# Weight pieces and context rows fetched on GpSimd's queue in the cross stage, and rounded in later slots

## The chip, the cores and the metric

The kernel runs on one core of a Trainium2 chip. A core has TensorE (matmuls into PSUM), VectorE, ScalarE, GpSimd, and SyncE (SP), which here only issues DMAs; the engines run by themselves and meet at semaphores. DMAs issued by SP and by GpSimd are moved by the same 16 DMA engines. The metric is the device time of one execution in microseconds (us). Runs of the kernel before took 1236.08, 1238.08 and 1243.37 us, a median of 1238.08.

## The reference

A decoder layer over x, 16 sequences of 128 rows and 512 columns, in float32:

```python
x = x + attn(layernorm(x))            # 16 query heads of 128, one key/value head, causal, rotary
x = x + xattn(layernorm(x), ctx)      # 8 heads of 16 over the 512 positions, band of 64 either way
x = x + ffn(layernorm(x))             # quantised linear layers with a gate

# xattn, per sequence: x is used as (128 features, 512 positions)
q, k, v = split(x.T @ w_in.T + b_in)
p = softmax(where(band, q @ k.T / sqrt(16), -big))
y = relu((p @ v) @ w_out.T + b_out).T * ctx      # ctx: the context rows of this sequence
out = w_ct.T @ y + b_ct

# ffn: both weight matrices are quantised to -1, 0, 1
scale = 1 / max(mean(abs(w)), 1e-5)
wq = clip(round(w * scale), -1, 1) / scale
```

## The kernel before, in words

The kernel has three stages: attention (to about 622 us of the span), the cross stage (to about 1022 us), and the feed-forward stage. Every stage is a software pipeline over the 16 sequences, written out by hand.

The cross stage (`cross`, L953 on) runs `step(b)` for b from -3 to 18 on each engine, and in each step 8 slots, s = 0 to 7. One step does different work for several sequences: maximum scores of sequence b + 1, shifted scores and exponentials of sequence b, attention values and their sums for b - 1, output projection and gate for b - 2, projections to q and k for b + 3, the update of x for b - 3. In each slot TensorE computes one unit of maximum scores into the PSUM tile `Sm` (L1024, L1032), for which VectorE must have read the unit before, and one unit of shifted scores into `Se`. VectorE takes the maxima of `Sm` (`maxima`, L1292) at the head of each slot and then does what else the slot holds: the update of x in slot 0 (L1339), two shuffles in slot 3 (L1347), the normalised input and the first half of the head values in slot 4 (L1276, L1308), the second half in slot 5, and the rests of q and k in slots 6 and 7 (L1282). ScalarE makes the exponentials (L1130).

The maxima go through TensorE (a transposition), ScalarE and VectorE to GpSimd, which splits them into three bfloat16 parts (L1191, L1193), and SP writes them as three rows into the tile Q (L1249; in the trace `Q<-x_m`), where the shifted scores read them: the rows of one half are awaited in slot 0, those of the other in slot 4 (`m_in`). q and k are also kept as three bfloat16 parts: SP writes them to HBM (`q_parts`, `k_parts`, L1234) and spreads them into Q and K (L1241). SP's order in a step is: context row for b - 2 (L1254), spread q, keep k, rows of maxima of the second half, spread k, rows of maxima of the first half, keep q, weight piece b + 1 (`load_piece`, L58 and L60). Each waits for its own semaphore, and what stands behind it waits as well.

Beside this the stage quantises the weights of the feed-forward stage. They are cut into 12 pieces (`PIECES`: 8 of the gate matrix, 128 x 1408, and 4 of the down matrix, up to 128 x 1536). Piece n is fetched into one of the two `w_stage` buffers, VectorE multiplies it by the inverse scale and adds a large number, which rounds it (`offset`, L1316), ScalarE takes the number off and writes it as bfloat16 (L1181), and VectorE clips it to -1 and 1 (`clip`, L1322). In the kernel before, piece b is offset in step b in slot 1, rounded by ScalarE in step b in slot 2, and clipped in step b + 1 in slot 2. The steps in which a piece is offset are 0 to 11.

GpSimd's order in a step is: low part of k (L1197), maxima parts of the second half, gate of b - 2 times the context row (L1213), maxima parts of the first half, attention values times their scales (L1218), low part of q, sum of the two halves (L1224). The context row is in one buffer, `ctxb`.

## Time and profile before

| | |
|---|---|
| Median of three runs | 1238.08 us (1236.08 to 1243.37) |
| Profiled execution | 1235.82 us |
| its span | 1234.0 us |
| TensorE, matmuls | 1035.4 us busy, 84% |
| VectorE | 813.1 us, 66% |
| ScalarE | 647.5 us, 52% |
| GpSimd | 640.5 us, 52% |
| Mean granted clock of TensorE | 0.945 of full speed |
| Weight pieces in the cross stage, issue to landing | 5.1 us (gate), 7.4 us (down), medians |
| Two fetches of 1024 KB each, issued back to back on GpSimd's queue in attention | 5.2 and 7.2 us to landing |

Busy time is how long an engine ran instructions; the rest of the span it waited. In a pipeline like this one the busy shares don't say what sets the time. For that one takes a step, lists the engine's instructions in order of time, and looks at what each one waited for. Times below are us from the start of the span. Names with L are lines of the kernel before.

### The profile page before, as it was taken

To read this page: it belongs to the slowest core of one execution; us is meant where nothing else is said; L and a number is where in the kernel's file an instruction comes from. 1 tells how busy PE (TensorE), PEld (TensorE's weight loads), DVE (VectorE), ACT (ScalarE), POOL (GpSimd) and SP (SyncE) were. 2 spreads that over 40 slices of the span, in tenths; PEclk is the share of its full clock that TensorE was granted. 3 is DMA by queue.
4 is the path that set the end of the run, shared out by engine and by line. 5 is a ranking of instruction groups with operands and counts; after the bars stand their busy time and mean duration, and the time that the engine had idled before them with its cause. 6 is when DMAs were issued, how large, how long until landed. Compare 5 with 4: busy or idle time off the path is not lost. (4 is left out here: it accounts for less than half of the span.)

```text
span 1234.0 us, 25423 instructions
## 1 busy us (share of the span) xinstructions
PE 1035.4 (84%) x9604; PEld 774.9 (63%) x9604; DVE 813.1 (66%) x1487; ACT 647.5 (52%) x1188; POOL 640.5 (52%) x584
## 2 busy tenths in 40 slices
PE   5689999999999999999635888989899954777675
PEld 5578887888888888887413666656566631333332
DVE  7678776666666666576334667676666645888884
ACT  5555545455454545556512566666556542455553
POOL 3665666566565657566315143434334334566653
PEclk9899999999999999999867899999999976899998
DMA  9043643233233332346336666665755200000000
GB/s 348 21 172 122 246 166 120 110 138 136 81 131 133 136 113 97 133 160 211 134 75 153 149 168 164 168 160 135 187 130 135 60 19 32 18 17 25 25 25 27
DMA packets 51135, 147.57 MB, mean 120 GB/s; under 512 B 10448, under 2 KB 24272, under 8 KB 39760
## 3 DMA queue, kind: packets, MB, share of 16 engines
q1 hardware_dynamic: 42288, 86.93, 25.3%
q0 software_dynamic: 8064, 58.72, 13.0%
q8 instruction: 75, 1.23, 0.4%
q10 hardware_dynamic: 672, 0.40, 0.1%
q14 instruction: 36, 0.29, 0.1%
HBM read 120.46 MB, written 25.17 MB: 118 GB/s over the span
## 5 line engine op out<-in xcount | busy, mean ns | idle before, releaser
L1292 DVE TENSOR_REDUCE mx<-Sm 128x4 f32<-128x768 f32 x128 | 122.4, 956 | 87.7 <-PE Sm L1032 87.2
L1130 ACT ACTIVATE x_ex<-Se 128x768 f32<-128x768 f32 x128 | 103.1, 805 | 116.4 <-PE Se L1032 116.0
L282 PE MATMUL Qb<-a_xTh,WqH 128*128 128x256 f32 x512 | 146.3, 286 | 3.1 <-DVE a_vl L800 3.0
L283 PE MATMUL Qb<-a_xTl,WqH 128*128 128x256 f32 x512 | 145.6, 284 | 0.0
L284 PE MATMUL Qb<-a_xTh,WqL 128*128 128x256 f32 x512 | 145.4, 284 | 0.0
L627 POOL TENSOR_TENSOR a_pr<-a_pr_plain,a_ph 128x512 fp32r<-128x512 f32 x64 | 83.6, 1307 | 110.2 <-ACT a_ph L447 110.0
L740 DVE TENSOR_TENSOR a_turned<-Qb,sinS 64x512 f32<-64x512 f32 (+1 forms) x144 | 94.9, 659 | 62.6 <-PE Qb L284 45.1
L609 POOL TENSOR_TENSOR a_ql<-a_rot,a_qh 128x512 fp32r<-128x512 f32 x64 | 83.9, 1315 | 98.4 <-ACT a_qh L467 98.2
L459 ACT ACTIVATE Lb<-Lb 128x512 f32<-128x512 f32 x64 | 37.2, 582 | 170.4 <-PE Ob L354 170.4
L367 PE MATMUL Yb<-a_WoH,a_oH 128*128 128x512 f32 x256 | 103.2, 403 | 5.5 <-POOL a_oN L605 5.5
L282 PEld LDWEIGHTS Qb<-a_xTh,WqH 128*128 128x128 f32 x512 | 98.6, 193 | 6.9 <-issue 2.4
L369 PE MATMUL Yb<-a_WoH,a_oN 128*128 128x512 f32 x256 | 101.3, 396 | 0.0
L368 PE MATMUL Yb<-a_WoL,a_oH 128*128 128x512 f32 x256 | 101.1, 395 | 0.0
L283 PEld LDWEIGHTS Qb<-a_xTl,WqH 128*128 128x128 f32 x512 | 98.6, 193 | 2.4
L284 PEld LDWEIGHTS Qb<-a_xTh,WqL 128*128 128x128 f32 x512 | 98.6, 193 | 0.0
L605 POOL TENSOR_TENSOR a_oN<-a_oN_plain,a_oH 128x512 fp32r<-128x512 f32 x64 | 84.9, 1327 | 3.0 <-ACT a_oH L439 3.0
L1024 PE MATMUL Sm<-band,ident_b 128*64 128x256 bf16 x512 | 54.9, 296 | 31.2 <-DVE mx L1292 18.2
L756 DVE TRANSPOSE_TENSOR_REDUCE a_rmax<-Sb 128x16 f32<-128x512 f32 x64 | 45.6, 712 | 51.6 <-PE Sb L334 51.5
L1024 PEld LDWEIGHTS Sm<-band,ident_b 128*64 128x64 bf16 x512 | 19.0, 111 | 90.3 <-issue 46.1
L636 POOL TENSOR_TENSOR Dg<-ident,a_negm 32x512 fp32r<-32x512 f32 x64 | 66.5, 1039 | 13.2 <-DVE a_negm L763 10.5
L1578 POOL TENSOR_TENSOR f_hg<-f_h,g 128x512 f32<-128x512 f32 (+1 forms) x48 | 56.0, 1181 | 32.3 <-DVE f_h L1658 32.3
L1482 PE MATMUL Gb<-gateQ,f_xqT 128*128 128x512 bf16 (+1 forms) x192 | 48.0, 374 | 29.1 <-DVE f_h L1658 27.4
(202 smaller groups left out, 2841.4 us busy)
## 6 DMA issues: line engine op xcount, KB each, us to landing
a_WoH<-wo_parts POOLq DMA_DIRECT2D x28, 1024.0 KB, 5.2
a_WoL<-wo_parts POOLq DMA_DIRECT2D x28, 1024.0 KB, 7.2
K<-k_parts SPq DMA_DIRECT2D x32, 256.0 KB, 4.8
q_parts<-x_qp SPq DMA_DIRECT2D x16, 384.0 KB, 3.0
Q<-q_parts SPq DMA_DIRECT2D x16, 384.0 KB, 5.6
k_parts<-x_kp SPq DMA_DIRECT2D x16, 384.0 KB, 7.4
a_w_stage<-in_gateT SPq DMA_DIRECT2D x8, 704.0 KB, 4.5
x_w_stage<-in_gateT SPq DMA_DIRECT2D x8, 704.0 KB, 5.1
```

The lines of the kernel that those rows point to most:

```text
L282: pe.matmul(out, w_hi(k), xTh[:, k, :], start=(k == 0), stop=False)
L283: pe.matmul(out, w_hi(k), xTl[:, k, :], start=False, stop=False)
L284: mm = pe.matmul(out, w_lo(k), xTh[:, k, :], start=False, stop=(k == KD - 1))
L367: pe.matmul(Yb[s % 2][:, :], high, WoH[u % 2][:, i, :], start=(i == 0), stop=False)
L368: pe.matmul(Yb[s % 2][:, :], high, WoL[u % 2][:, i, :], start=False, stop=False)
L369: mm = pe.matmul(Yb[s % 2][:, :], low, WoH[u % 2][:, i, :], start=False, stop=(i == HG - 1))
L605: pool.tensor_tensor(oL[:, s % 2, :], oN[:, s % 2, :], oH[:, s % 2, :].bitcast(F32), ALU.subtract).then_inc(oL_ready, 1)
L609: pool.tensor_tensor(rot_dst(False, True, par, r), rbuf(par, r)[:, 0:rot_width(r)], rot_dst(True, False, par, r).bitcast(F32), ALU.subtrac ...
L627: pool.tensor_tensor(pl[:, :], pr[:, :], ph[:, :].bitcast(F32), ALU.subtract).then_inc(pl_ready, 1)
L740: dve.tensor_tensor(dst[to:to + hi - lo, 0:width].rearrange("p (j c) -> p j c", c=P), bank[lo:hi, 0:width].rearrange("p (j c) -> p j c", c=P),
L1130: act.activation(ex[:, (PAIRS * b + p) % RING, 4 * hf * WIN:4 * (hf + 1) * WIN].rearrange("p (j c) -> p j c", j=2), Se[:, :, 0:2 * WIN], A ...
L1292: dve.tensor_reduce(mx[:, half, at:at + 4].rearrange("p (j a) -> p j a", j=2), Sm[:, :, 0:2 * WIN].rearrange("p j (a c) -> p j a c", a=2), ...
```

## The change

The fetches of the weight pieces and of the context rows are issued by GpSimd at the end of its step in place of SP. The context row for sequence b - 1 is fetched at the end of GpSimd's step b, where SP fetched the one for b - 2 at the start of its step b. The piece is offset in step b in slot 3 in place of slot 1, rounded by ScalarE in step b + 1 in slot 2 in place of step b, and clipped in step b + 2 in place of b + 1. The work on each piece is the same.

```diff
--- before.py
+++ after.py
@@ -50,14 +50,14 @@
 MAGIC = 1.5 * 2.0 ** 23
 
 
-def load_piece(sp, dram, n, to):
+def load_piece(eng, dram, n, to):
 
     i, lo, hi = PIECES[n]
     if i == 0:
         k, at = divmod(lo, 2 * F)
-        return sp.dma_start(to[:, 0:hi - lo], dram["gateT"][k * P:(k + 1) * P, at:at + hi - lo])
+        return eng.dma_start(to[:, 0:hi - lo], dram["gateT"][k * P:(k + 1) * P, at:at + hi - lo])
     src = dram["downT"][lo // D * P:hi // D * P, :].rearrange("(k p) n -> p k n", p=P)
-    return sp.dma_start(to[:, 0:hi - lo].rearrange("p (k n) -> p k n", n=D), src)
+    return eng.dma_start(to[:, 0:hi - lo].rearrange("p (k n) -> p k n", n=D), src)
 
 
 def norm_scales(nc, t, again, ctx):
@@ -1175,10 +1175,11 @@
                         for hh in range(2):
                             act.activation(rl[:, hh, :], rl[:, hh, :], ACT.Exp, scale=-1.0,
                                            bias=t["live"][:, hh:hh + 1]).then_inc(rl_ready, 1)
-                    if s == 2 and 0 <= b < len(PIECES):
-                        i, lo, hi = PIECES[b]
-                        wait(act, w_rounded, b + 1)
-                        act.activation((t["gateQ"], t["downQ"])[i][:, lo:hi], w_stage[b % 2][:, 0:hi - lo], ACT.Copy,
+                    n = b - 1
+                    if s == 2 and 0 <= n < len(PIECES):
+                        i, lo, hi = PIECES[n]
+                        wait(act, w_rounded, n + 1)
+                        act.activation((t["gateQ"], t["downQ"])[i][:, lo:hi], w_stage[n % 2][:, 0:hi - lo], ACT.Copy,
                                        bias=-MAGIC).then_inc(w_whole, 1)
 
             steps(step)
@@ -1222,6 +1223,11 @@
                     wait(pool, oU_scaled, b)
                     wait(pool, out_full, b - 1)
                     pool.tensor_tensor(oN[:, :], oU[:, 0, :], oU[:, 1, :], ALU.add).then_inc(oN_ready, 1)
+                    wait(pool, y_ready, b - 2)
+                    pool.dma_start(ctxb[:, :], dram["ctx"][b - 1]).then_inc(ctx_in, 16)
+                if 0 <= b + 1 < len(PIECES):
+                    wait(pool, w_whole, b)
+                    load_piece(pool, dram, b + 1, w_stage[(b + 1) % 2]).then_inc(w_in[(b + 1) % 2], 16)
 
             steps(step)
 
@@ -1249,9 +1255,6 @@
                     sp.dma_start(to, m3[half][:, k, :]).then_inc(m_in[half], 16)
 
             def step(b):
-                if real(b - 2):
-                    wait(sp, y_ready, b - 2)
-                    sp.dma_start(ctxb[:, :], dram["ctx"][b - 2]).then_inc(ctx_in, 16)
                 if real(b + 2):
                     spread("q", Q, Q_RUNS, b + 2, q_kept, q_in)
                     keep("k", kp, b + 2, k_low, k_in, K_IN, k_kept)
@@ -1263,10 +1266,6 @@
                     maxima_rows(b + 1, 0)
                 if real(b + 3):
                     keep("q", qp, b + 3, q_low, q_in, Q_IN, q_kept)
-                if 0 <= b + 1 < len(PIECES):
-                    wait(sp, w_whole, b)
-                    load_piece(sp, dram, b + 1, w_stage[(b + 1) % 2]).then_inc(w_in[(b + 1) % 2], 16)
-
             steps(step)
 
         @block.vector
@@ -1357,10 +1356,10 @@
                         rest(qp, qr, 0, b + 3, q_high, q_low, q_rest)
                     if s == 7 and real(b + 3):
                         rest(kp, kr, 1, b + 3, k_high, k_low, k_rest)
-                    if s == 1 and 0 <= b < len(PIECES):
+                    if s == 3 and 0 <= b < len(PIECES):
                         offset(b)
-                    if s == 2 and 0 <= b - 1 < len(PIECES):
-                        clip(b - 1)
+                    if s == 2 and 0 <= b - 2 < len(PIECES):
+                        clip(b - 2)
                     if b >= B - 1 and s % 2 == 1:
 
                         first = (b - B + 1) * 4 + s // 2
```

## Rows read from the trace of the kernel before

**Rows 1.** Busy time by stretch: start:end, length, busy time (instructions), clock, DMA share, GB/s.

```profile
694.14:929.13 234.99, 210.05 (x3782) 144.36 (x3782) 160.31 (x262) 148.30 (x219) 89.62 (x98) 0.98 0.65 159
929.13:948.27 19.14, 18.79 (x346) 12.91 (x346) 13.74 (x24) 12.30 (x19) 8.29 (x10) 1.00 0.62 140
```

**Rows 2.** Tile w_stage, whole span: who waited (us, times), and time to landing.

```profile
  DVE x_w_stage L1316: 25.7, 12
...
DMA to landing us min/median/max: 4.6/5.1/7.8
```

**Rows 3.** Waits by total, 672 to 968 us: who, for whom: us, times, longest.

```profile
PEld Se L1024 <- DMA Q<-x_m: 12.3, 12, 2.3
```

**Rows 4.** VectorE in order of time, step 4: start, duration, operation, [idle before <-releaser].

```profile
758.52 0.96 DVE L1292 TENSOR_REDUCE mx<-Sm 128x4 f32<-128x768 f32 x1 [1.04 <-PE Sm L1032]
...
760.71 0.95 DVE L1316 TENSOR_SCALAR x_w_stage<-x_w_stage,w_inv 128x1408 f32<-128x1408 f32 x1 [1.12 <-DMA x_w_stage<-in_gateT]
761.58 0.95 DVE L1292 TENSOR_REDUCE mx<-Sm 128x4 f32<-128x768 f32 x1
...
763.76 0.96 DVE L1292 TENSOR_REDUCE mx<-Sm 128x4 f32<-128x768 f32 x1 [0.79 <-PE Sm L1032]
...
771.69 0.96 DVE L1292 TENSOR_REDUCE mx<-Sm 128x4 f32<-128x768 f32 x1 [0.70 <-PE Sm L1032]
```

**Rows 5.** VectorE in order of time, step 12 (no offset): slots 1, 3, 4 and 6.

```profile
932.02 0.96 DVE L1292 TENSOR_REDUCE mx<-Sm 128x4 f32<-128x768 f32 x1 [1.27 <-PE Sm L1032]
...
937.26 0.96 DVE L1292 TENSOR_REDUCE mx<-Sm 128x4 f32<-128x768 f32 x1 [1.64 <-PE Sm L1032]
...
939.51 0.96 DVE L1292 TENSOR_REDUCE mx<-Sm 128x4 f32<-128x768 f32 x1
...
943.82 0.96 DVE L1292 TENSOR_REDUCE mx<-Sm 128x4 f32<-128x768 f32 x1
```

**Rows 6.** VectorE: the offset of step 0; slots 1, 3 and 6 of step 10.

```profile
678.36 0.95 DVE L1316 TENSOR_SCALAR x_w_stage<-x_w_stage,w_inv 128x1408 f32<-128x1408 f32 x1 [3.10 <-DMA x_w_stage<-in_gateT]
...
885.81 0.96 DVE L1292 TENSOR_REDUCE mx<-Sm 128x4 f32<-128x768 f32 x1 [1.04 <-PE Sm L1032]
...
893.40 0.96 DVE L1292 TENSOR_REDUCE mx<-Sm 128x4 f32<-128x768 f32 x1 [0.35 <-PE Sm L1032]
...
901.50 0.96 DVE L1292 TENSOR_REDUCE mx<-Sm 128x4 f32<-128x768 f32 x1 [0.25 <-PE Sm L1032]
```

**Rows 7.** TensorE's weight loads: shifted scores in slot 4 of step 4; values in step 11.

```profile
767.61 0.14 PEld L1024 LDWEIGHTS Se<-band,ident_b 128*64 128x64 bf16 x4 [1.26 <-DMA Q<-x_m]
...
914.42 0.12 PEld L1075 LDWEIGHTS XY<-x_ex,Vw 64*32 64x32 f32 x1 [2.59 <-issue]
```

**Rows 8.** SP's DMA issues in order of time, step 4.

```profile
755.94 0.48 SPq L58 DMA_DIRECT2D x_w_stage<-in_gateT  x1
...
758.53 1.25 SPq L1241 DMA_DIRECT2D Q<-q_parts  x3
...
760.38 3.07 SPq L1249 DMA_DIRECT2D Q<-x_m  x3
```

**Rows 9.** DMA issues by line, 757:765 and 932:939 us: count, KB, median us to landing.

```profile
Q<-x_m SPq DMA_DIRECT2D x3, 4.0 KB, 5.6
...
Q<-x_m SPq DMA_DIRECT2D x3, 4.0 KB, 3.6
```

**Rows 10.** GpSimd in order of time, attention: one of its DMA issues.

```profile
317.27 0.60 POOL L600 DMA_DIRECT2D a_WoH<-wo_parts  x1
```

**Rows 11.** GpSimd in order of time: low part of k in step 4; last gate.

```profile
758.25 1.16 POOL L1197 TENSOR_TENSOR x_kp<-x_kr,x_kp 128x512 bf16<-128x512 f32 x1 [1.59 <-ACT x_kp L1145]
...
1016.91 1.26 POOL L1213 TENSOR_TENSOR x_gate<-x_gate,x_ctxb 128x512 f32<-128x512 f32 x1 [2.99 <-ACT x_gate L1158]
```

**Rows 12.** Busy time by stretch, step 3: the last column is GB/s.

```profile
738.00:740.00 2.00, 2.00 (x70) 1.55 (x67) 0.80 (x3) 0.81 (x1) 1.21 (x3) 1.00 1.04 392
740.00:744.00 4.00, 2.83 (x50) 1.29 (x48) 2.24 (x3) 3.10 (x3) 0.00 (x0) 1.00 1.02 185
```

## The prediction

> **What bounds the kernel now.** I read the page's busy shares first. No engine fills the 1234.0 us span, so the kernel must be read by stage, and the change lies in the cross stage alone. There I cut the span at the first maxima of every step. Eleven steps that fetch and round a weight piece take 234.99 us, 21.36 us each; the next one, with no offset left, takes 19.14 [rows 1]. So a piece costs about 2.2 us a step. The reader is to see that this is more than its work on VectorE: the offset holds it 0.87 us, from 760.71 to 761.58 [rows 4].
>
> Who waits for whom comes next. VectorE waits 25.7 us, 12 times, for the piece's transfer ahead of the offset [rows 2]; TensorE waits 12.3 us for the rows of maxima, "Q<-x_m" [rows 3]. Is the 25.7 on the path? In step 4 the maxima of slot 1 starts at 758.52, the offset has 1.12 us of waiting before it, and the maxima of slot 3 starts at 763.76: 5.24 us from slot 1 to slot 3 [rows 4]. In the step without a piece these two are at 932.02 and 937.26: 5.24 us too [rows 5]. TensorE (attention values, output projection) sets that length, so a wait of 1.1 us is hidden. Pieces land 4.6 to 7.8 us after their issue [rows 2], and where one is late it shows: step 10 goes from 885.81 to 893.40, 7.59 us, 2.35 more [rows 6].
>
> But the next thing in line is late as well. In slot 4 TensorE starts the shifted scores only when three rows of maxima have landed: in step 4 at 767.61, after 1.26 us of waiting [rows 7], 9.09 after slot 1's maxima; slot 6's maxima follows 4.08 us later, at 771.69 [rows 4]. Slot 1 to slot 6 is 13.17 us in step 4, and 11.80 in the step without a piece [rows 5]. These rows of maxima leave SP from 760.38 on, behind the piece (755.94), the context rows and Q's spread (758.53) [rows 8]. They land 5.6 us after issue, against 3.6 in the step without a piece [rows 9]: they are the tail of a backlog. So most piece steps are paced by the rows of maxima, and the offset's wait lies beside that.
>
> **The change part by part.** My measure is slot 1 to slot 6; the rest of a step (19.14 - 11.80 = 7.34 us) holds nothing that changes.
>
> *The offset leaves slot 1.* Its wait and its 0.87 us go from between slots 1 and 2. By the equal 5.24 us this gives 0 in a typical step and the excess where the piece was late.
>
> *The offset enters slot 3, behind the two shuffles.* There VectorE has no gap: slot 3 is 937.26 to 939.51, 2.25 us, with no idle time before the next maxima [rows 5]. It grows to 3.12. TensorE's maximum scores of slot 5 wait for slot 4's maxima, and the next shifted scores and a projection stand behind them; with that I get 1.07 at slot 6 (bounds 0.87 and 1.3). A step whose rows of maxima are in time then takes 11.80 + 1.07 = 12.87 us. This is a floor; a step's length is the larger of it and "rows landed + 4.08". With rows as now, step 4 stays at 13.17: the 0.87 is hidden under the wait for them. If that cover goes, the floor is left, and it is still 0.3 below step 4.
>
> *The wait for the piece, now in slot 3.* The offset would start at 763.76 + 2.25 = 766.0. Issued at 755.94 as now, the piece has 10 us; GpSimd issues it some 1.3 us later, which leaves 8.8 against the slowest landing of 7.8: no wait. ScalarE's rounding and the clip take pieces a step older; their work stays in slot 2, beside TensorE's 5.24 us as now, so they cost 0. ScalarE's own waits for the offset go; they lay beside VectorE's.
>
> *GpSimd issues two more DMAs at the end of its step.* In attention one of its issues takes 0.60 us [rows 10]; two are 1.20. In the cross stage it idles 1.59 us at this place, until ScalarE gives k's middle part at 758.25 [rows 11]. So 1.2 fits with 0.4 to spare. Behind the issues stand k's low part (SP's k_parts and K's spread wait for it) and the maxima's low parts (the rows of slot 4). A down piece has 384 runs in place of 128, and no row shows such an issue from GpSimd: bounds 0.6 and three times that, 1.8. At 1.8, k's low part slips 0.8 us, but k_parts queue behind Q's spread anyway; I take 0. The waits ahead of the issues (gate done, piece rounded) are met slots before.
>
> *SP is rid of two issues* of some 0.5 us (the piece's is 0.48 [rows 8]). Next on SP is Q's spread at 758.53, which waits for q_parts to land: 0.
>
> *When do the rows of maxima land?* This decides. The bytes are the same. For later: piece and context leave about 1 us later, the engines may idle more, and the tail moves out; bound 0.5 us. For earlier: in step 3 piece and context move at 392 GB/s, and Q's spread behind them at 185 [rows 12]. It no longer stands behind the piece; if they overlap, the slow phase is filled. The bound is that the piece costs nothing, 2.0 us earlier, as in the step without one [rows 9]. I take 0.4 earlier, nearer to the row with the same bytes. Eight steps (2 to 9) are bound by these rows: 8 x 0.4 = 3.2 us.
>
> The Trainium skill, "DMA: Bandwidth & Descriptors", section "Issuing engines are not separate DMA queues", speaks against this: DMAs of all issuers run on the same 16 engines, and a second issuer only saves sequencer time. By that this term is 0 and the sum 3.4. Rows 9 agree in so far as the tail follows the bytes ahead of it; no row of the cross stage has both queues.
>
> *Steps on their own.* Step 0 waited 3.10 us for its piece [rows 6]; then its rows of maxima bind: 1.6 gained. Step 1: its rows came early, before the context fetches begin, and the floor is above it: 0.4 lost. Step 10: 885.81 to 901.50 is 15.69 [rows 6]; its rows bind at about 14.4, 1.3 gained. Step 11: TensorE stood 2.59 us for nothing that the profile shows [rows 7]; if that doesn't recur up to 2 are gained, I take 1.2. Tail: the last context row is fetched behind GpSimd's last sum, which ends at 1016.91 - 2.99 = 1013.92 [rows 11]. With some 3.1 us to landing it is in at 1017.0, and its gate started at 1016.91: 0.3 lost (0 to 1).
>
> **Sum.** 3.2 + 1.6 - 0.4 + 1.3 + 1.2 - 0.3 = 6.6 us. The profiled execution took 1235.82 (span 1234.0 and 1.8 around it), so 1229.2 there. The median of the runs shown is 1238.08, 2.3 above it, and 1238.08 - 6.6 = 1231.5 is my forecast: 0.53% faster, just over the 0.5% (6.2 us) that a measurement of this kernel can tell from no change.
>
> **The rivals.**
> - *The waits move, the bytes don't: gain 3.4, 1234.7.* The rows of maxima land as now. For: equal bytes ahead of them. Against: two transfers with different rates [rows 12] may overlap.
> - *All the waiting comes back: gain 12.8 and more, 1225.* Needs rows of maxima 2 us earlier, so that every piece step falls to the floor: 12.87 + 7.34 = 20.2 in place of 21.36, times 11. For: the step without a piece. Against: the bytes are in flight in the same window.
> - *Slower: the second queue pushes the rows of maxima back.* The place is slot 4 of each piece step. If the piece, started 1 us later, takes turns with Q's spread and k_parts to the end, the last of SP's rows comes later. From 0.4 us on it eats the 3.4 (9 steps); at 1.2 it costs 10.8 - 3.4 = 7.4 us: 1245.5. For: these rows come last of all now. Against: no byte is added.
> - *The change doesn't do what it says:* pieces from GpSimd's queue land after 8.8 us and VectorE waits in slot 3, 1 to 2 us for each. Its 1 MB fetches in attention land 5.2 and 7.2 us after issue (the table of the profile), the second behind the first; a piece is 0.7 MB. Counted in the slower share.
>
> **How the numbers follow.** Forecast (gain 4 to 11) 0.50, of which 0.37 lies past 6.2; unmoved rows 0.25, all within; full return 0.08, faster; later rows and late pieces 0.17, of which 0.15 is slower past 6.2. Faster 0.45, within 0.5% 0.40, slower 0.15. The range goes from 1223 (full return) to 1242 (rows of maxima 0.8 later). The likeliest case's own range is 1227 to 1234.
>
> **What would show it.** Right: VectorE's waits for w_stage gone; slot 1 to 3 at 5.24 in step 10; slot 3 at 3.1 in place of 2.25; TensorE still waiting for "Q<-x_m", landing about 5.2 us after issue in piece steps; k's low part on GpSimd still released by ScalarE. Wrong: piece steps near 20.2 with no wait for "Q<-x_m" (full return); that wait beyond 15 us, or VectorE waiting for w_stage in slot 3 (slower); a slot 3 of 2.25, which would mean that the offset isn't in VectorE's way.

## The result: 1.4% slower, and the profile after

The changed kernel took 1259.41 us (median; 1250.56 to 1262.11), the kernel before on the same chip 1240.72: a ratio of 1.0139, 95% interval 1.0073 to 1.0205. The forecast was 1231.5, and the range ended at 1242. The profiled execution took 1262.11 us, with a span of 1260.3, 26.3 more than before. The two medians are only 18.7 apart: the profiled execution is the slowest of the changed kernel's four and before's, at 1235.82, lies below all its others, so what follows from the two traces is a little large. Two executions in all the series below stand far out, which nothing here explains (3438.93 us in E6's, 2028.58 us of the kernel before in the series of E1, E2, E3 and E5), and the ratios leave them out.

First the same cut by steps as in [rows 1]: the eleven steps in which a piece is offset, and the next one. Columns: start:end, length, busy time of PE, PEld, DVE, ACT, POOL, granted clock, DMA share, GB/s.

```profile
697.51:952.83 255.32, 222.91 (x3782) 152.54 (x3782) 164.90 (x261) 151.50 (x219) 102.08 (x119) 0.90 0.60 146
952.83:972.14 19.31, 18.60 (x346) 12.94 (x346) 13.86 (x23) 13.17 (x20) 8.87 (x11) 1.00 0.62 139
```

Eleven steps took 234.99 us before and take 255.32 now: 21.36 and 23.21 each. The step without a piece is as it was (19.14, 19.31). So 20.3 of the 26.3 us lie in the steps with a piece; 3.4 came before step 1 and 2.6 behind step 11. Of the 3.4, 2.8 lie before step 0. It starts at 672.41 before and at 675.25 now, but F4 below, which fetches everything on SP, has 675.16, so this part can't be put down to the change. TensorE's mean clock in the eleven steps fell from 0.98 to 0.90, and its busy time for the same 3782 matmuls rose from 210.05 us [rows 1] to 222.91. The DMA engines' share fell as well, from 0.65 to 0.60, but over a longer stretch: 0.65 x 235 and 0.60 x 255 are both 153 us of work. They aren't fuller.

The waits over the whole span (engine, line, for whom; us, times, longest):

```profile
PEld Se L1024 <- DMA Q<-x_m: 38.3, 16, 5.3
...
DVE x_w_stage L1315 <- DMA x_w_stage<-in_downT: 2.1, 2, 1.3
DVE x_w_stage L1315 <- DMA x_w_stage<-in_gateT: 0.7, 1, 0.7
```

VectorE's waiting for pieces went from 25.7 us [rows 2] to 2.8. TensorE's waiting for the rows of maxima went from 12.5 (12.3 in the stretch of [rows 3]) to 38.3. The wait moved and grew.

A step is best compared slot by slot: the time from the head of each slot (the maxima on VectorE) to the next, as a mean over steps 1 to 11, read from VectorE's rows in order of time.

| us | 0 | 1 | 2 | 3 | 4 | 5 | 6 | 7 | step |
|---|---|---|---|---|---|---|---|---|---|
| before | 2.70 | 4.00 | 2.56 | 2.40 | 2.59 | 2.69 | 2.23 | 2.19 | 21.36 |
| after | 2.68 | 2.38 | 2.83 | 3.98 | 3.13 | 3.80 | 2.23 | 2.19 | 23.21 |

Slots 1 and 2 gave 1.35 us, slot 3 took 1.58, slot 4 took 0.54 and slot 5 took 1.11. Step 3 shows how. VectorE and GpSimd, in order of time:

```profile
744.53 0.96 DVE L1291 TENSOR_REDUCE mx<-Sm 128x4 f32<-128x768 f32 x1 [1.04 <-PE Sm L1032]
...
749.77 0.96 DVE L1291 TENSOR_REDUCE mx<-Sm 128x4 f32<-128x768 f32 x1 [1.54 <-PE Sm L1032]
...
751.76 1.26 POOL L1214 TENSOR_TENSOR x_gate<-x_gate,x_ctxb 128x512 f32<-128x512 f32 x1 [5.38 <-ACT x_gate L1158]
751.91 1.86 DVE L1315 TENSOR_SCALAR x_w_stage<-x_w_stage,w_inv 128x1408 f32<-128x1408 f32 x1
753.69 0.94 DVE L1291 TENSOR_REDUCE mx<-Sm 128x4 f32<-128x768 f32 x1
...
760.28 0.96 DVE L1291 TENSOR_REDUCE mx<-Sm 128x4 f32<-128x768 f32 x1 [2.29 <-PE Sm L1032]
```

Slot 1 to slot 3 is 749.77 - 744.53 = 5.24 us, the length of [rows 4, 5]. Slot 3 is 3.92 in place of 2.25: the offset takes 1.86 us where it took 0.95 [rows 4], and it starts 0.15 us after GpSimd's multiplication of the gate by the context row. GpSimd is done at 753.02, the offset 0.75 later.

TensorE in the same step, weight loads with a wait, and two projections of equal shape:

```profile
754.62 0.14 PEld L1024 LDWEIGHTS Se<-band,ident_b 128*64 128x64 bf16 x4 [2.46 <-DMA Q<-x_m]
...
757.12 2.08 PE L1060 MATMUL XY<-x_x,wqk 128*128 128x512 f32 x2
...
760.69 1.12 PE L1060 MATMUL XY<-x_x,wqk 128*128 128x512 f32 x2
```

The shifted scores of slot 4 start 754.62 - 744.53 = 10.09 us after slot 1's maxima, where step 4 before had 9.09 [rows 4, 7]. TensorE stood for 2.46 us, and 2.5 us on, a projection takes 2.08 where the next one takes 1.12. The cut of the span at these two projections has the granted clock (the column before the last two):

```profile
757.12:759.20 2.08, 2.08 (x6) 0.58 (x6) 0.83 (x3) 2.08 (x5) 0.60 (x2) 0.50 0.86 181
760.69:761.81 1.12, 1.12 (x6) 0.36 (x6) 1.12 (x2) 0.81 (x1) 0.99 (x1) 1.00 0.02 2
```

The first ran at the lower clock level (1.2 GHz for 2.4). That is slot 5's growth. Cut at slot 5 of steps 1 to 11, the granted clock is 0.51 to 0.71 in ten of them now and 1.00 in step 2; before, it is 1.00 in all but step 8 (0.61), the one step with a wait of 2.30 us.

SP and GpSimd issue their DMAs at these times, and the DMA list for 742 to 756 us gives the median time to landing:

```profile
743.21 0.54 POOL L58 DMA_DIRECT2D x_w_stage<-in_gateT  x1
744.27 1.15 POOL L1198 TENSOR_TENSOR x_kp<-x_kr,x_kp 128x512 bf16<-128x512 f32 x1 [0.52 <-ACT x_kp L1145]
...
744.08 1.69 SPq L1247 DMA_DIRECT2D Q<-q_parts  x3
...
746.40 2.33 SPq L1255 DMA_DIRECT2D Q<-x_m  x3
```

```profile
x_w_stage<-in_gateT POOLq DMA_DIRECT2D x1, 704.0 KB, 6.9
...
k_parts<-x_kp SPq DMA_DIRECT2D x1, 384.0 KB, 8.2
...
Q<-x_m SPq DMA_DIRECT2D x3, 4.0 KB, 6.4
```

Before, the piece was issued 0.08 us into step 4 (755.94, with the step starting at 755.86), now 1.34 us into step 3, whose start is 741.87. The rows of maxima are issued at the same point of the step, 1.87 us after slot 1's maxima (1.86 before [rows 4, 8]), and land 6.4 us later in place of 5.6 [rows 9].

One step is not the mean. Reading issue and landing of these rows in the same way in each of steps 1 to 11 gives, as a mean, how long after slot 1's maxima they have landed:

| landed, us after slot 1's maxima | |
|---|---|
| piece from SP at the turn of the step: before, E1, E4, F3 | 8.02, 8.14, 8.13, 8.19 |
| piece from GpSimd at the end of its step: E2, the change, E3 | 8.45, 8.63, 8.63 |
| rows ahead of the kept k parts: F2, E12, F1 | 7.29, 7.24, 7.94 |

(E and F are the experiments below.) The change makes the rows 0.6 us later, of which GpSimd's fetches make 0.5 (E1 to the change, E4 to E3) and the later slots 0.1.

### The profile page after: what moved, and what is told of

Its sections match the earlier page's. It is cut to its first block and busy times, and to the rows that moved or that the text cites. A ratio compares the mean times of both kernels' runs of the same rounds, so it can differ in the third digit from the quotient of the medians.

```text
span 1260.3 us, 25423 instructions
## 1 busy us (share of the span) xinstructions
PE 1053.2 (84%) x9604; PEld 786.0 (62%) x9604; DVE 817.1 (65%) x1487; ACT 650.2 (52%) x1188; POOL 655.6 (52%) x612
## 3 DMA queue, kind: packets, MB, share of 16 engines
q0 software_dynamic: 11264, 71.57, 15.9%
## 5 line engine op out<-in xcount | busy, mean ns | idle before, releaser
L1024 PE MATMUL Se<-band,ident_b 128*64 128x256 bf16 x512 | 55.0, 297 | 43.0 <-DMA Q<-x_m 35.6
L636 POOL TENSOR_TENSOR Dg<-ident,a_negm 32x512 fp32r<-32x512 f32 x64 | 66.5, 1039 | 12.9 <-DVE a_negm L763 10.0
```

The source lines that it names most:

```text
L1024: pe.matmul(at, t["ident_b"][:, TS * hh:TS * hh + TS], masks, start=True, stop=True, skip_group_check=True)
```

## The experiments

A *spread* below is SP's copy of the q or k parts into Q or K, *kept* parts are those it writes to HBM. Theory: the rows of maxima, 12 KB behind over 1 MB (Q's spread and the kept k parts), pace the steps. What VectorE waited for the piece covered the wait for them. The piece on the second queue makes them later, and the idle time costs TensorE its clock. Rivals: the longer offset in slot 3 is the loss; or the second queue as such.

"Rows" below means TensorE's wait for `Q<-x_m` over the whole span (us, times). Each ratio is to the kernel before on the same chip. The six kernels in which only the fetching engine and the offset's place differ make a table:

| fetched by | offset in slot 1 | in slot 3 | in slot 1 of the next step |
|---|---|---|---|
| SP | before, 1.000 | E1 1.0079 | E4 1.0021 |
| GpSimd | E2 1.0195 | the change 1.0139 | E3 1.0123 |

**E1, the later slots alone**

```diff
-    if s == 1 and 0 <= b < len(PIECES):
+    if s == 3 and 0 <= b < len(PIECES):
         offset(b)        # rounding n = b - 1, clip(b - 2) as in the change; fetches on SP
```

> The later slots alone; all fetches stay on SP. Theory: the offset in slot 3 falls on GpSimd's gate multiplication and takes 1.86 us in place of 0.95, so slot 3 is 3.9 us (2.25 before); the rows of maxima land as before (shifted scores of slot 4 start 9.1 to 9.6 us after slot 1's maxima), TensorE's wait for them stays near 12 us, so the step is bound by the longer slot 3 only a little above the old length: 0 to 6 us slower than before. Rival (the slots are harmless, all of the loss is the queue): slot 3 is 3.1 us and the time is 3 us or more below before.

1251.07 us, ratio 1.0079 (1.0044 to 1.0113). Slot 3 is 3.70 and the rows 24.6 us, 15 times, twice the 12.5 of before over the whole span. The theory was missed on both: 11 us above before where it had 0 to 6, and the wait twice the 12 that it had. The rows land when they did (8.14 us after slot 1's maxima, 8.02 before), and still the wait doubles. Moving the offset alone costs: the cover of the wait for the rows is gone, and slot 3 is longer.

**E2, GpSimd's fetches alone**

```diff
+    wait(pool, y_ready, b - 2)          # end of GpSimd's step; SP's two fetches removed
+    pool.dma_start(ctxb[:, :], dram["ctx"][b - 1]).then_inc(ctx_in, 16)
+    load_piece(pool, dram, b + 1, w_stage[(b + 1) % 2]).then_inc(w_in[(b + 1) % 2], 16)
```

> The queue alone; the offset is in slot 1 again, rounding and clip as before. Both theories: pieces land later (7 us after an issue that is 1.3 us later), VectorE waits about 4 us for them in slot 1 of each piece step, over 40 us in all, and slot 1 to 3 grows from 5.2 to over 7 us: 20 to 30 us slower than before. Theory: the rows of maxima, which land about 1 us later, then lie beside that wait, so TensorE's wait for them is under 15 us. Rival (the queue pushes these rows back by several us): that wait stays at 30 us or more.

1262.47 us, ratio 1.0195 (1.0126 to 1.0264). VectorE waits in slot 1:

```profile
DVE x_w_stage L1314 <- DMA x_w_stage<-in_gateT: 27.3, 8, 5.6
DVE x_w_stage L1314 <- DMA x_w_stage<-in_downT: 22.2, 4, 7.4
```

49.5 us in place of 25.7 [rows 2], slot 1 at 6.23 us, and the rows are down to 8.8: under so long a wait they are hidden. All this is as expected. So the piece lands later in the step when GpSimd fetches it, and this is the dearer half. The two halves don't add: alone the later slots (E1) cost 0.8%, while from E2 to the change they seem to give 0.6% back (the intervals overlap).

**E3, the change with the offset in slot 1 of the next step**

```diff
-    if s == 3 and 0 <= b < len(PIECES):
-        offset(b)
+    if s == 1 and 0 <= b - 1 < len(PIECES):
+        offset(b - 1)
```

> The change, with the offset of a piece in slot 1 of the step after its fetch has landed (one step later than before) in place of slot 3; fetches on GpSimd's queue. Theory: the offset takes 0.95 us again and slot 3 2.25, the rows of maxima still land late (10 us after slot 1's maxima), TensorE waits for them 30 us or more and its clock falls in several steps: half of the loss stays, 6 to 14 us above before. Rival (the collision with the gate is the cause, the queue harmless): at or below before, with a wait for these rows of about 12 us.

1257.07 us, ratio 1.0123 (1.0055 to 1.019). The offset is back at 0.93 us and slot 3 at 2.32, 1.66 less than in the change, yet slot 4 is 4.72 and the rows 39.0. The time is 17 us above before, more than the 6 to 14 expected. The longer offset is not the loss: the wait behind it takes its room.

**E5, the change with GpSimd's gate after its first maxima parts**

```diff
+                if real(b + 1):
+                    maxima_low(b + 1, 0)
                 if real(b - 2):
                     wait(pool, gate_ready, b - 1)     # ... gate times context row
-                if real(b + 1):
-                    maxima_low(b + 1, 0)
```

> The change, but GpSimd multiplies the gate with the context row after the low parts of the first half's maxima, so that it is idle while VectorE offsets in slot 3. Theory: the offset takes 0.95 us and slot 3 3.1 us in place of 3.9, while the rows of maxima land as late as in the change: 2 to 8 us faster than the change, still 8 us or more slower than before. Rival (the offset is slow in slot 3 for another reason, as the DMA traffic): it stays at 1.86 us.

1261.44 us, ratio 1.0157 (1.009 to 1.0223). The offset takes 0.93 us in slot 3, with nothing beside it on GpSimd, and slot 3 is 3.24 us, as expected; the rows are 42.1. The gain of 2 to 8 us over the change didn't come (the two can't be told apart). The same answer with the offset where the change has it.

**E4, fetches on SP, offset in slot 1 of the next step**

```diff
-    if s == 1 and 0 <= b < len(PIECES):
-        offset(b)
+    if s == 1 and 0 <= b - 1 < len(PIECES):
+        offset(b - 1)    # rounding n = b - 1, clip(b - 2)
```

> Both fetches stay with SyncE, as before; the offset of piece b-1 is made in slot 1 of the next step, the rounding in its slot 2, the clip a step later, so neither VectorE's wait for the piece nor the gate's multiplication lies beside the offset. Theory (the rows of maxima are the tail of the step's transfers and pace slot 4; what VectorE waited for the piece merely covered that wait): slots 1 to 3 shorten by over 2 us against before, slot 4 grows by nearly as much, TensorE idles there before its matmul of the maxima, the granted clock falls, and the steps' mean is 21.3 to 22.4 us against 21.36 before and 22.44 with the later slots alone: 1238 to 1252 us. Rival A (the offset beside the gate's multiplication was the whole loss): slot 3 at 2.4 us and nothing else grown, 1225 to 1235 us. Rival B (waits only cost where they end last, no clock loss): 1239 within 3 us.

1243.98 us, ratio 1.0021 (0.9996 to 1.0045), steps of 21.94: time and steps are in the theory's range, and not told apart from before. VectorE never waits for a piece, slot 1 falls from 4.00 to 2.31, but slot 2 grows from 2.56 to 3.53, so slots 1 to 3 lose 0.8 us and not over 2; slot 4 goes from 2.59 to 3.41 with the rows at 26.8. The same kernel with GpSimd's fetches, E3, is 1% slower. With the offset in slot 3 (E1) it is 0.6% slower: the longer slot 3 costs something where the rows are less late. One thing was in neither expectation. From E4's VectorE, GpSimd and SP in order of time:

```profile
739.98 0.96 DVE L1293 TENSOR_REDUCE mx<-Sm 128x4 f32<-128x768 f32 x1 [1.04 <-PE Sm L1032]
...
740.99 0.93 DVE L1317 TENSOR_SCALAR x_w_stage<-x_w_stage,w_inv 128x1408 f32<-128x1408 f32 x1
741.14 0.96 POOL L1192 TENSOR_TENSOR x_m<-x_mr,ones 32x64 bf16<-32x64 f32 x1 [0.27 <-DVE x_mr L1300]
...
742.50 2.01 SPq L1250 DMA_DIRECT2D Q<-x_m  x3
```

An offset that doesn't wait starts just ahead of GpSimd's part of the maxima, which then takes 0.96 us and not 0.31, and the rows leave 742.50 - 739.98 = 2.52 us after slot 1's maxima, not 1.86 [rows 4, 8]. The old wait had pushed the offset past it.

**E7, work for TensorE while it waits (the change otherwise)**

```diff
+                for _ in range(6 if s == 4 else 1):
+                    masked(Se, s)                       # mask matmuls of the scores
                 if s % 4 == 0:
                     wait(pe, m_in[s // 4], M_IN * (b + 1))
```

> The change, with TensorE's mask matmuls of the scores put ahead of its wait for the rows of maxima, and made six times over in slot 4 (the repeats write the same values, so what is computed is unchanged): TensorE has work while it waits. Theory (about 1.5 us of each step is the clock, which falls because TensorE idles over 2 us in slot 4): the granted clock of the steps rises from 0.86 to 0.93 towards 1.00, slot 5 goes from 3.8 towards 2.8 us, slot 4 is no more than 0.4 us longer, 1240 to 1252 us. Rival (the transfers alone set the steps and the clock's fall is covered): slots 4 and 5 together within 0.3 us of the 6.93 us of the change, 1257 to 1263 us.

1247.37 us, ratio 1.0057 (1.0033 to 1.0081), where the change has 1.0139. Step 3 of each kernel, the change first:

```profile
741.87:764.73 22.86, 20.19 (x346) 13.61 (x346) 15.41 (x25) 13.88 (x20) 9.46 (x12) 0.93 0.61 150
```

```profile
743.47:763.73 20.26, 19.78 (x366) 13.92 (x366) 15.33 (x25) 13.54 (x20) 8.92 (x12) 1.00 0.65 168
```

In E7 the rows land as late as in the change (8.49 us after slot 1's maxima as a mean, 8.63 there). The granted clock is 1.00 in place of 0.93, slot 5 falls from 3.80 to 2.85 and slot 4 from 3.13 to 2.65; over steps 1 to 11 that is 23.21 to 21.67. Part of slot 4's gain is that the masks no longer stand behind the wait; this kernel doesn't tell the two apart there. Slot 5 has only the clock. So of the change's loss about 1 us a step is the clock.

**E6, SP fetches in the middle of its step (E4 otherwise)**

```diff
                 if real(b + 1):
                     maxima_rows(b + 1, 0)
+                ...                      # ctx b - 1, piece b + 1 on SP; old places removed
                 if real(b + 3):
                     keep("q", qp, b + 3, q_low, q_in, Q_IN, q_kept)
```

> As the kernel with the offset in the next step's slot 1 and both fetches on SyncE, but SyncE issues the context row and the next piece in the middle of its step, behind the rows of maxima of the first half and ahead of the kept Q, where the transfers stood idle before. Theory (the rows of maxima come late because they queue behind piece and context row): TensorE's wait for them (12.5 us over 13 places before, 38.3 us over 16 after the change) falls to under 12 us, slot 4 stays near 2.6 us, and the steps of 21.36 us become 19.2 to 20.5: 1215 to 1232 us. Rival A (the rows are late for another reason: the Q spread, the k parts or VectorE's own maxima): the waits stay above 20 us and the time within 5 us of the kernel of the later slots, 1245 to 1256 us. Rival B (the piece now holds up the rows of maxima of the second half or the last rows of the step): a wait of the same size in slots 6 and 7 or in the next slot 0, 1235 to 1250 us.

1245.63 us, ratio 1.0033 (1.0003 to 1.0063): the theory's time was missed (1215 to 1232), and the rows (30.8, 17 times) are as rival A had them. SP in order of time says why; the step starts at 757.80:

```profile
756.04 0.58 SPq L1264 DMA_DIRECT2D x_ctxb<-in_ctx  x1
756.66 0.43 SPq L58 DMA_DIRECT2D x_w_stage<-in_gateT  x1
757.45 0.38 SPq L1235 DMA_DIRECT2D q_parts<-x_qp  x1
762.39 1.25 SPq L1242 DMA_DIRECT2D Q<-q_parts  x3
763.74 0.38 SPq L1235 DMA_DIRECT2D k_parts<-x_kp  x1
764.17 2.07 SPq L1250 DMA_DIRECT2D Q<-x_m  x3
```

The middle of SP's list comes at the end of the step: the first half's rows are out only at 756. The kept q stands behind nearly 1 MB, the Q spread comes 4.6 us into the step, and the rows of maxima, in line behind it, at 764.17.

**E8, GpSimd fetches in the middle of its step (E3 otherwise)**

```diff
                 if real(b + 1):
                     maxima_low(b + 1, 0)
+                ...                      # ctx b - 1, piece b + 1 on GpSimd; old places removed
```

> As the kernel with GpSimd's fetches and the offset in the next step's slot 1 (1257.07 us), but GpSimd issues the context row and the piece in the middle of the step, behind the low parts of the first half's maxima. Theory (it is when the bytes move that counts, not which engine's queue carries them): close to the same with SyncE's queue in the middle of the step, within 6 us of it, at most 1236 us. Rival (the second queue itself delays SyncE's small rows, whenever it carries bytes): no better than 1250 us, with TensorE's wait for the rows of maxima still above 30 us.

1237.13 us, ratio 0.997 (0.9944 to 0.9995), 1.1 above the theory's bound, 8.5 from E6 where it had 6, and far from the rival's 1250. On the same queue, 20 us below E3: it isn't the second queue that costs, but when it carries the piece. Nor are pieces slow from it: here the gate pieces land 5.1 us after issue (median), as in before from SP. Slot 4 is 2.22 and slot 5 2.26. The delay went to the rows of the other half: the rows still cost 32.2 us, now mostly in slot 0, which is 5.11.

**E12, rows of maxima ahead of the kept k parts (E4 otherwise)**

```diff
+                if real(b):
+                    maxima_rows(b, 1)
                 if real(b + 2):
                     keep("k", kp, b + 2, k_low, k_in, K_IN, k_kept)
-                if real(b):
-                    maxima_rows(b, 1)
```

> The kernel with both fetches on SyncE and the offset in the next step's slot 1 (1243.98 us), with one order changed: SyncE issues the rows of maxima of the second half ahead of the kept k parts (384 KB) and not behind them. Theory (the rows of maxima are late because they are the tail of what is already in the transfers' rings): their landing, 4.5 us in the median there, falls by about a microsecond, TensorE's wait for them from 26.8 to under 15 us in all, and the time to 1228 to 1238 us. Rival A (only the Q spread and the piece ahead of them count, or the rows leave before the k parts get going anyway): within 3 us of 1243.98. Rival B (the k parts, now issued about a microsecond later, make the K spread and the next step's rows later still): slower, 1246 us or more.

1224.85 us, ratio 0.9881 (0.9832 to 0.9929), better than expected. The rows fall from 26.8 to

```profile
PEld Se L1024 <- DMA Q<-x_m: 13.4, 13, 2.7
```

by one exchange of two issues: 384 KB no longer stand in front of 12 KB.

**E9, the piece behind the K spread, the context row behind the first half's rows (E4 otherwise)**

```diff
                     spread("k", K, K_RUNS, b + 2, k_kept, k_in)
+                ...                      # piece b + 1 on SP
                 if real(b + 1):
                     maxima_rows(b + 1, 0)
+                ...                      # ctx b - 1 on SP
```

> As the kernel in which SyncE fetches in the middle of the step (1245.63 us), but the piece goes directly behind the K spread, ahead of the wait for the first half's maxima, and only the context row behind that: the piece moves while SyncE would wait, and the kept Q of the next step is not held up. Theory: the Q spread of the next step is again issued about 2.2 us into the step and not up to 4.6 us, the rows of the second half's maxima with it; TensorE's wait for them falls from 30.8 to under 15 us and the time to 1222 to 1236 us. Rival A (the piece then lands across the first half's rows of maxima): waits in slot 0 as in the kernel with GpSimd's fetches in the middle (5.1 us in place of 2.7), 1237 to 1245 us. Rival B (the Q spread and the k parts alone make the rows late): 1241 to 1249 us.

1226.38 us, ratio 0.9899 (0.9856 to 0.9941). The time is as expected, the rows (20.4) fell less than that. E6's fault is mended: the piece moves while SP waits for the first half's rows.

**E10, both; E11, both with E7's masks**

> Both of the two edits above in one kernel: the piece behind the K spread, the context row behind the first half's rows, and the second half's rows ahead of the kept k parts. Theory: the gains add, as each takes other bytes from in front of the same rows: 1218 to 1230 us, the steps at 19.2 to 20.2 us, with slot 4 near 2.3 us. Rival (the step is bound by the sum of its transfers, 0.64 of the span's share, wherever they stand): no better than the better of the two, 1234 us or more.

> The same with the mask matmuls of the scores put ahead of TensorE's wait for the rows of maxima and made six times over in slot 4 (the repeats write the same values). Theory (an idle TensorE costs clock beside the wait itself): as far as slot 4 still waits over 2 us, slot 5 falls from over 3 us to 2.8 or less: 2 to 8 us below the same without it. Rival (no waits over 2 us are left, or the repeats lie on the path): within 2 us of it, or slower.

E10: 1222.42 us, ratio 0.9871 (0.983 to 0.9912); E11: 1225.83, 0.9908 (0.988 to 0.9936). E10's time is as expected, its steps are 20.44 us (19.2 to 20.2 expected). The gains don't add: slot 4 is down to 2.21, but slot 0 is 4.10, where the first half's rows now come late. In E11 slot 4 is 2.60 in nearly every step and slot 5 2.80 (2.17 in E10); with little left to wait for, the six repeats lie on the path. The rival had that; by the intervals E11 and E10 can't be told apart.

**F1, the change with E12's order**

```diff
+                if real(b):
+                    maxima_rows(b, 1)
                 if real(b + 2):
                     keep("k", ...)        # GpSimd's fetches, offset in slot 3
```

> The change itself, with one order of SyncE's turned: the rows of maxima of the second half are issued ahead of the kept k parts. Theory (the change is slower because these rows land later behind more bytes; the offset beside the gate's multiplication is covered by that wait): taking 384 KB from in front of them gives back 10 to 20 us, 1240 to 1250 us, with TensorE's wait for them falling from 38.3 to under 25 us and slot 4 from 3.13 to under 2.6; what stays above before is slot 3, now 1.6 us longer in every step with nothing to cover it. Rival (the second queue itself or the longer offset costs the time): within 5 us of 1259.4 us.

1243.0 us, ratio 1.0031 (1.0006 to 1.0056), in the theory's range. One exchange on SP takes the ratio from 1.0139 to 1.0031, over three quarters of the loss. The rows are 29.5 (the theory had under 25), slot 4 is 2.63, slot 5 2.91 in place of 3.80; slot 3 stays 3.97. Two of its steps, 785.28 to 805.54 and the one after, take 20.26 us each, under before's mean of 21.36.

**F2, the kernel before with E12's order**

> The kernel before, with that one order turned. Theory: TensorE's wait for the rows was 12.5 us in all and part of it reappears as VectorE's wait for the pieces (25.7 us), which this edit doesn't shorten: 2 to 10 us below before, 1227 to 1236 us. Rival (all of the 15 to 19 us that the order gave in the kernel with the offset in the next step come back here too): 1218 to 1225 us.

1229.73 us, ratio 0.9942 (0.9912 to 0.9971): the rows fall from 12.5 to 5.5 us, the waits for pieces stay at 15.9 and 9.4. As the theory had it. E12, with the same order and the offset moved, is at 0.9881: once the rows come earlier, taking away the wait for the piece seems to pay as well (the intervals just overlap).

**F3, only the context row from GpSimd (E4 otherwise)**

```diff
+                    wait(pool, y_ready, b - 2)
+                    pool.dma_start(ctxb[:, :], dram["ctx"][b - 1]).then_inc(ctx_in, 16)
```

> The offset in the next step's slot 1, the context row fetched by GpSimd at its step's end and the piece by SyncE: half way between the kernel with both on SyncE (1243.98 us) and the one with both on GpSimd (1257.07 us). Theory A (GpSimd fetches the row of the next output while SyncE's queue carries the piece: 256 KB move to a time when rows of maxima are under way): 1247 to 1253 us. Theory B (it is the piece of 704 KB on the other queue that shares the transfer engines with the small rows): within 3 us of 1244 us.

1242.28 us, ratio 1.0045 (1.0017 to 1.0072): theory B. With the context row and the piece from GpSimd the ratio is 1.0123 (E3), with the context row alone it can't be told from E4's, and the rows are 26.4 as there (26.8). E3 differs from it in the piece alone. So it is the piece, issued by GpSimd and some 1.3 us later.

**F4, the kernel before with E10's order on SP**

```diff
-                if real(b - 2):
-                    ...                                        # ctx b - 2
                 if real(b + 2):
                     spread("q", Q, Q_RUNS, b + 2, q_kept, q_in)
-                    keep("k", kp, b + 2, k_low, k_in, K_IN, k_kept)
                 if real(b):
                     maxima_rows(b, 1)
                 if real(b + 2):
+                    keep("k", kp, b + 2, k_low, k_in, K_IN, k_kept)
+                if real(b + 2):
                     spread("k", K, K_RUNS, b + 2, k_kept, k_in)
+                if 0 <= b + 1 < len(PIECES):
+                    ...                                        # piece b + 1, removed from the end
                 if real(b + 1):
                     maxima_rows(b + 1, 0)
+                if real(b - 1):
+                    ...                                        # ctx b - 1
```

> The kernel before with its own slots for offset, rounding and clip, and SyncE's order alone turned as in the fastest kernel so far (1222.42 us): rows of maxima ahead of the kept k parts, the piece behind the K spread, the context row behind the first half's rows. Theory (order of the transfers is what counts, and a piece fetched that early has landed before VectorE asks for it): VectorE's wait for the pieces under 3 us, within 3 us of 1222.4 us. Rival (the later slots are needed, since the offset of slot 1 still waits): 1228 to 1238 us.

1220.92 us, ratio 0.9853 (0.9805 to 0.9901): the lowest median, as expected (by the intervals not told apart from E10), and the offset is still in slot 1 of its own step. The ten steps from step 2 on, and SP in step 4 (from 754.03):

```profile
714.29:917.83 203.54, 191.66 (x3442) 131.36 (x3443) 146.40 (x240) 134.42 (x200) 90.02 (x92) 0.98 0.67 164
```

```profile
756.55 1.26 SPq L1241 DMA_DIRECT2D Q<-q_parts  x3
760.31 2.22 SPq L1249 DMA_DIRECT2D Q<-x_m  x3
762.62 0.53 SPq L1234 DMA_DIRECT2D k_parts<-x_kp  x1
767.23 1.70 SPq L1241 DMA_DIRECT2D K<-k_parts  x4
768.97 0.42 SPq L58 DMA_DIRECT2D x_w_stage<-in_gateT  x1
770.36 1.78 SPq L1249 DMA_DIRECT2D Q<-x_m  x3
```

A step is 20.4 us, no wait for a piece is in the list any more, and the clock is 0.98. What is left is in slot 0 (4.07 us): the first half's rows, issued at 770.36, behind the piece of 768.97.

## Why the prediction was wrong, step by step

- *"So most piece steps are paced by the rows of maxima, and the offset's wait lies beside that."* Right, and the key: E12, F1 and F2 all move the time by turning one order, after which these rows land 0.7 to 0.9 us earlier. But "eight steps (2 to 9)" was a little much: TensorE waits for the rows in seven of them, and in two of these (3 and 9) only 0.34 and 0.28 us.
- *The offset leaves slot 1: 5.24 us from slot 1 to slot 3.* Right to the hundredth in step 3.
- *Slot 3 grows to 3.12.* It is 3.92. The term took the offset's 0.87 for granted in its new place. It didn't look at what GpSimd does there: the gate's multiplication. The size was off by 0.8 us, but in the changed kernel it costs next to nothing that can be measured (E3, E5).
- *"I take 0.4 earlier"* for the rows of maxima. **This is the step that failed.** They land later: 0.8 in step 3 after the same issue, 0.6 as the mean of steps 1 to 11 (8.02 to 8.63 us after slot 1's maxima). Over the steps in which TensorE waits for them, the shifted scores of slot 4 start 9.8 us after slot 1's maxima before (seven of steps 2 to 9) and 10.4 after (ten of steps 2 to 11). The text had seen that the piece would start about 1 us later, and set against this a gain from overlap that no row showed. [Rows 12] spoke against it: the DMA share (the column before GB/s) is 1.04 in the fast phase and 1.02 in the slow one, so the engines were as busy at 185 GB/s as at 392, and there was no idle time to fill. The third rival had the place right (slot 4) and the point from which it decides (0.4 us). At 0.6 later it gives 9 x 0.6 - 3.4 = 2.0 us, and the steps lost 20.3. Most of the rest is the next term.
- *No price for the clock.* The sum took every TensorE duration as it was. This term, put at nothing, is the larger part of the loss. Behind waits of 1.8 to 4.2 us for the rows the granted clock of slot 5 is 0.51 to 0.71 in ten of the eleven steps: slot 5 went from 2.69 to 3.80, 1.11 x 11 = 12.2 us, and TensorE was busy 12.9 us longer for the same matmuls. E7 shows it: its slot 5 is 2.85, so 0.95 x 11 = 10.5 us come back there, and its ratio is 1.0057.
- *Slots 1 and 2 give nothing* was taken for typical steps, and 1.3 and 1.2 us for steps 10 and 11. They gave 1.35 us a step, but slot 4 can't use it: it is the rows that end last there. Steps 10 and 11, for which it had gains, grew by 1.6 and 0.5 us (22.80 to 24.37, 23.18 to 23.70).
- *The wait for the piece, now in slot 3: none.* Nearly right: 2.8 us in 3 places. The piece takes 6.9 us in step 3, the down pieces up to 10.1, over the 7.8 of [rows 2]; the room of some 9 us just held.
- *GpSimd's two issues hide in its 1.59 us [rows 11].* Right: they take 0.60 and 0.54 (0.71 to 0.78 for a down piece), and the low part of k is still released by ScalarE, after 0.52.
- *The tail, 0.3 lost.* It is 0.1: the last gate starts 4.38 us after the start of GpSimd's last sum (1038.26 to 1042.64), 4.25 before (1012.66 to 1016.91). But from step 12 to this gate 2.0 us more went by (87.78 to 89.81), which the sum doesn't have.

The rule of the Trainium skill, "DMA: Bandwidth & Descriptors", section "Issuing engines are not separate DMA queues" (all issuers' DMAs run on the same 16 engines and interleave), stood against the overlap, and the trace agrees: it gives no gain. The loss is beyond it. The section "Queues, rings and completion order" of the same page of the Trainium skill says that an engine takes turns between the queues it has work for. By that the small rows at the tail of SP's queue share each turn with a piece that is still under way; the trace shows the piece in flight until 743.21 + 6.9 = 750.1, in the same window as SP's 1 MB, but not the single turns, so this cause of the later landing is argued, not shown. Shown is that it is the piece (F3) and its moment (E8).

Open: how much of the 0.5 us that GpSimd's fetches cost these rows is the later start of the piece and how much the taking of turns; no kernel issued it from GpSimd at SP's old time, or from SP 1.3 us later.

## What to carry to other kernels

Before you remove a wait, find what else would have been late behind it: two waits side by side cost one, and taking the visible one away shows the other. Where small DMAs that an engine waits for share the transfer engines with large ones, order them first; here one exchange of two issues gave 0.6, 1.1 and 1.4% in three kernels, while moving the offset alone (E1, E4) gave nothing. And price TensorE's waits with its clock: here waits of some 2 to 4 us cost about 1 us a step once more, in the matmuls behind them.

## What was not expected of the hardware

- *VectorE beside GpSimd.* The offset (SBUF to SBUF, float32, a gate piece) takes 0.93 to 0.95 us alone and 1.86 when it starts 0.15 us after a GpSimd operation of 1.26 us. In the other order GpSimd's small operation takes 0.96 and not 0.31. Whoever comes second waits for the first: 753.02, the end of GpSimd's, plus 0.95 is 753.97, and the offset ended at 753.77. The Trainium skill, "SBUF — State Buffer", section "Who interferes with whom", says this of VectorE's fast modes: the second to issue is blocked until the first is through. The trace agrees within 0.2 us.
- *TensorE's clock.* After 2.46 us of waiting the projection took 2.08 us for 1.12; in a kernel where TensorE had matmuls to do meanwhile (E7) the clock of the whole step was 1.00.
- *A stall of TensorE for nothing that the profile shows.* TensorE stands 0.4 to 3.4 us in the middle of the attention values in a few steps, as in [rows 7]: between 690 and 930 us 4.5 us in 4 places before, 7.0 in 4 in E1, 4.9 in 3 in E4, 6.4 in 4 in E12, 7.6 in 4 in F2, 3.3 in 3 in F3. In all these SP fetches the piece at the turn of its step. Where GpSimd fetches it, or SP behind the first half's rows or the K spread, it is 0 to 0.6 us (0.26 in the change). An example from E4:

```profile
920.28 0.52 PE L1075 MATMUL XY<-x_ex,Vw 64*32 64x128 f32 x2 [2.49 <-issue]
```

  E4's DMA share is 1.07 from 916 to 919 us. What it waits for isn't shown, and no run tested it.
